# Row maxima, block masks and their spreading matrix padded to 128 on one Trainium2 core

## The chip, the cores and the metric

The kernel runs on one core of a Trainium2 chip. The metric is the time of one execution on the device in microseconds (us), here the median of several runs. The core has five engines that work from queues of their own and wait for each other through semaphores: TensorE (PE; its weight loads are a line of their own, PEld), VectorE (DVE), ScalarE (ACT), GpSimd (POOL) and SyncE (SP), which here only issues transfers (DMA).

## The reference

Inputs are x and ctx, both 8 x 256 x 256 (batch, tokens, width), so 2048 tokens. Four layers follow each other, each added to x:

```python
x = x + softmax(q k^T / sqrt(256)) v          # 16 heads, q = layernorm(x), k = v = ctx
x = x + moe(layernorm(x))                     # 64 experts, 8 per token
x = x + causal_attention(layernorm(x), ctx)   # 16 heads, Wq, Wk, Wv, Wo
x = x + block_ffn(layernorm(x))               # below
```

The last layer has 1024 hidden units in 16 blocks of 64. A router picks 4 of the 16 blocks for each token; hidden units of the others count as zero:

```python
mask = zeros(n, 16).at[rows, top_k(softmax(xf @ router_w.T + router_b), 4)].set(True)
h = relu(where(mask, xf @ w1.T + b1, 0))
y = where(mask, h, 0) @ w2.T + b2
```

## The kernel before

The run has five stages: `prepare` (layer norm and splitting of operands into bf16 parts), a first `attention` ("a0") with the routing of the experts worked in beside it (class `Route`), `experts`, a second `attention` ("a1", causal) with the sum over experts, the query projection and the beginning of the last layer worked in beside it (classes `Combine` and `FirstGroup`), and `finish`, the last layer.

**Attention.** One function builds both. It goes through 16 steps, two per batch, each with 8 heads. For a head PE computes the scores twice: queries by keys (L472, in a1 with a mask added at L475), of which DVE takes the row maxima (L568, in a1 L565), and two steps later keys by queries (L489, L492), from which ACT makes exponentials (L627). The maximum enters this second product as two extra rows of its operand `qst`. For that `cut` on DVE writes the negated maxima of a step as bf16, in a high part (L581) and a rest (L584), into `maxparts`, 16 columns (2 parts of 8 heads) for each half of the queries. PE turns them with two transposes, one per half (`turn_maxima`, L531): the weights are 128 rows by 16 columns, the moving operand is the bf16 identity. The result `max_t` has 16 rows; ACT copies it to `maxrows` (L651), and SP moves it by DMA into `qst`. The two transposes stand in PE's queue after head 4 of each step. PE then multiplies exponentials by values (L512, 32 columns of the array at a time) and turns the outputs (L523). The order of all queues is written out by hand in the functions `step` of each engine; the classes beside the attention hang their work at given heads of given steps.

**The last layer.** The tokens are in four groups of 512. For each group `close_blocks` on DVE (in a1, for the first group, `close`) turns the router's logits into `closed`: 0 for a chosen block and -1e30 for the others, 128 tokens x 16 blocks for each of 4 tiles, fp32. PE turns these with four transposes (`turn_masks`, L1999, and L1799 in a1) into 16 rows in PSUM, which ACT copies to `closed_t` as bf16 (L2056). Then, for each of 8 slices of 128 hidden units, `hidden` adds up in a PSUM bank the products of `w1` with the tokens (L2007; two calls, of which each shows as two fp32 matmuls in the trace) and the product of `spread` with `closed_t` (L2010): `spread` is a 16 x 128 matrix of zeros and ones that gives every hidden unit its block's mask. ACT applies relu with the bias (L2064), and for each tile `output` multiplies by `w2` (L2018). `spread` and the weights are loaded by SP in step 16 of a1 (`FirstGroup.sync`), and every engine of `finish` begins by waiting for them.

Of the kernel before, what the change touches and what calls it, by code (L numbers as in the profile page):

```python
# [7 lines left out]
F32 = mybir.dt.float32  # L8
BF16 = mybir.dt.bfloat16
I32 = mybir.dt.int32  # L10
ALU = mybir.AluOpType
# [3 lines left out]
P = 128  # L15
BATCH, SEQ, D = 8, 256, 256
# [5 lines left out]
HSTEP = HEADS // 2  # L22
# [313 lines left out]
def attention(nc, k, name, q_stack, k_stack, values, scale, causal, out, side):  # L336
# [13 lines left out]
    with ExitStack() as ctx:  # L350
# [10 lines left out]
        maxparts = sb("maxparts", [P, 2, 2, 2, HSTEP], BF16)  # L361
# [9 lines left out]
        max_t = ps[0:2 * HSTEP, 6, SEQ:SEQ + P].bitcast(BF16)  # L371
# [8 lines left out]
        cut_step = sem("cut_step")  # L380
        recips = sem("recips")
# [36 lines left out]
        with nc.Block() as block:  # L418
# [41 lines left out]
            def _(pe):  # L460
# [65 lines left out]
                def turn_maxima(st):  # L526
# [3 lines left out]
                    for j in range(2):  # L530
                        last = pe.transpose(max_t[:, j * P:(j + 1) * P],  # L531
                                            maxparts[:, u % 2, j].rearrange("p a s -> p (a s)"), k.ident_b[:])
# [25 lines left out]
            def _(dve):  # L558
                side.vector_first(dve)
# [11 lines left out]
                def cut(st):  # L571
# [9 lines left out]
                    nc.vector.tensor_copy(maxparts[:, v, :, 0, :], negmax[:, v]).then_inc(cut_step, 1)  # L581
                    per = 3 if causal else 1
                    dve.wait_ge(cut_step, per * h + per)
                    nc.vector.tensor_tensor(maxparts[:, v, :, 1, :], negmax[:, v], maxparts[:, v, :, 0, :], ALU.subtract).then_inc(max_ready, 1)  # L584
# [32 lines left out]
            def _(act):  # L617
# [27 lines left out]
                def copy_maxima(st):  # L645
# [5 lines left out]
                    nc.scalar.copy(maxrows[:, u % 2, :], max_t).then_inc(max_copied, 1)  # L651
# [803 lines left out]
class Combine:  # L1455
# [74 lines left out]
    def gpsimd(self, pool):  # L1530

        pool.wait_ge(self.xn_ready, 4)
# [173 lines left out]
class FirstGroup:  # L1706


    def __init__(self, nc, k, ctx):
# [9 lines left out]
        self.spread = sb("spread", [BLOCKS, FC, P], BF16)  # L1719
# [10 lines left out]
        self.closed = sb("closed", [P, GT, BLOCKS], F32)  # L1730
        self.closed_t = sb("closed_t", [BLOCKS, 2, GT * P], BF16)
        self.early_in, self.w_in = ctx.enter_context(nc.semaphore("ff_early_in")), ctx.enter_context(nc.semaphore("ff_w_in"))

    def attach(self, sem, ps, free, divided):
# [3 lines left out]
        self.masks_ps = ps[0:BLOCKS, :]  # L1738
        self.a_turned, self.a_copied, self.a_ready, self.x_done = sem("ga_turned"), sem("ga_copied"), sem("ga_ready"), sem("gx_done")
        self.own, self.later, self.normal, self.turned, self.copied = sem("g_own"), sem("g_later"), sem("g_normal"), sem("g_turned"), sem("g_copied")  # L1740
        self.logits_ready, self.closing = sem("g_logits"), sem("g_closing")
        self.masks_ready, self.masks_turned, self.masks_copied = sem("g_masks"), sem("g_masks_turned"), sem("g_masks_copied")

    def sync(self, sp, n):
# [6 lines left out]
        if n == 16:  # L1751
            for tile, name in ((self.w1, "w1"), (self.b1, "b1"), (self.spread, "c_spread"), (self.w2, "w2")):
                load(tile, name, self.w_in)
            sp.dma_start(self.b2[:], self.k.dram["b2"].to_broadcast([P, D])).then_inc(self.w_in, 16)
# [108 lines left out]
    def close(self, dve):  # L1863
# [15 lines left out]
        nc.vector.tensor_tensor(self.closed[:], self.others[:], self.logits[:], ALU.is_equal).then_inc(self.closing, 1)  # L1879
# [363 lines left out]
```

## Time and profile before

| | us |
|---|---|
| runs | 1082.7, 1088.0, 1093.1; median 1088.0 |
| the profiled execution, first to last instruction | 1089.6 |
| of it: prepare | to 54 |
| first attention and routing | 54 to 299 |
| experts | 299 to 731 |
| second attention | 731 to 942 |
| last layer (`finish`) | 942 to 1089.6 |

In this execution PE is busy for 932.5 us, its weight loads for 635.0, DVE for 586.8, ACT for 375.0 and POOL for 526.0. A matmul's end is modelled in the profile and reaches into the next matmul, so the pace of PE is read from starts. "Idle before, issue" is time in which an engine waited for nothing that the profile shows.

### The profile page before, as it was taken

To read this page: it belongs to the slowest core of one execution; us is meant where nothing else is said; L and a number is where in the kernel's file an instruction comes from. 1 tells how busy PE (TensorE), PEld (TensorE's weight loads), DVE (VectorE), ACT (ScalarE), POOL (GpSimd) and SP (SyncE) were. 2 spreads that over 40 slices of the span, in tenths; PEclk is the share of its full clock that TensorE was granted. 3 is DMA by queue.
4 is the path that set the end of the run, shared out by engine and by line. 5 is a ranking of instruction groups with operands and counts; after the bars stand their busy time and mean duration, and the time that the engine had idled before them with its cause. 6 is when DMAs were issued, how large, how long until landed. Compare 5 with 4: busy or idle time off the path is not lost. (4 is left out here: it accounts for less than half of the span.)

```text
span 1089.6 us, 20810 instructions
## 1 busy us (share of the span) xinstructions
PE 932.5 (86%) x5679; PEld 635.0 (58%) x5686; DVE 586.8 (54%) x1789; ACT 375.0 (34%) x915; POOL 526.0 (48%) x511
## 2 busy tenths in 40 slices
PE   1188878877599999999999999954689999899998
PEld 1145444545467777777777777732467677465565
DVE  5678898856434444444444444426766867313320
ACT  3446555642322222222222222221245655412211
POOL 4400676776567777777777777722234400201010
PEclk9998898877889999999999999986889999999999
DMA  6764353201576566666666676536876741200000
GB/s 218 224 149 128 82 116 86 56 26 40 190 224 203 180 211 210 203 198 188 195 222 221 206 233 207 180 137 215 238 207 188 197 118 45 84 20 5 15 20 19
DMA packets 78872, 160.80 MB, mean 148 GB/s; under 512 B 18449, under 2 KB 44049, under 8 KB 76481
## 3 DMA queue, kind: packets, MB, share of 16 engines
q1 hardware_dynamic: 59264, 112.23, 35.0%
q0 software_dynamic: 19520, 47.41, 14.0%
q8 instruction: 55, 0.90, 0.4%
q14 instruction: 33, 0.26, 0.1%
HBM read 118.09 MB, written 41.22 MB: 146 GB/s over the span
## 5 line engine op out<-in xcount | busy, mean ns | idle before, releaser
L1318 PE MATMUL ex_ps<-ex_w_gu,ex_rows_t 128*128 x640 | 260.6, 489 | 0.6 <-ACT ex_rows_t L1385 0.6
L1285 POOL DMA_INDIRECT expert_outs<-ex_result,slot_places x160 | 157.5, 985 | 68.4 <-DVE ex_result L1431 55.9
L1280 POOL DMA_INDIRECT ex_rows<-moe_rows,slot_tokens x160 | 154.0, 962 | 55.3 <-issue 48.8
L894 POOL DMA_INDIRECT expert_lists<-rt_number,rt_idx x128 | 124.3, 971 | 102.9 <-DVE rt_idx L995 63.0
L1337 PE MATMUL ex_ps<-ex_w_down,ex_hidden_t 96*128 x640 | 166.5, 382 | 1.0 <-DVE ex_hidden_t L1423 1.0
L1391 ACT ACTIVATE ex_act_g<-ex_ps 128x192 f32<-128x192 f32 x160 | 53.0, 331 | 319.8 <-PE ex_ps L1318 319.8
L627 ACT ACTIVATE a_probs<-a_ps 128x512 f32<-128x512 f32 (+1 forms) x256 | 133.4, 540 | 83.2 <-PE a_ps L489 41.4
L472 PE MATMUL a_ps<-stacked_keys,a_qst 96*128 96x256 bf16 (+1 forms) x512 | 109.5, 286 | 36.7 <-DVE a_negmax L568 11.5
L1431 DVE TENSOR_SCALAR ex_result<-ex_ps,ex_rows 128x256 f32<-128x256 f32 x160 | 77.3, 483 | 94.0 <-PE ex_ps L1337 94.0
L1337 PEld LDWEIGHTS ex_ps<-ex_w_down,ex_hidden_t 96*128 96x128 f32 x640 | 108.6, 190 | 12.0 <-issue 2.3
L1318 PEld LDWEIGHTS ex_ps<-ex_w_gu,ex_rows_t 128*128 128x128 f32 x640 | 109.7, 192 | 9.8 <-issue 1.6
L1417 DVE TENSOR_TENSOR ex_hidden<-ex_act_g,ex_ps 128x192 f32<-128x192 f32 x160 | 56.6, 354 | 107.8 <-ACT ex_act_g L1391 107.8
L489 PE MATMUL a_ps<-a_qst,stacked_keys 98*128 98x256 bf16 (+1 forms) x512 | 105.4, 277 | 4.8 <-DMA a_qst<-a_maxrows 2.5
L568 DVE TENSOR_REDUCE a_negmax<-a_ps 128x2 f32<-128x512 f32 x128 | 84.9, 686 | 24.2 <-PE a_ps L472 23.2
L565 DVE TENSOR_REDUCE a_blockmax<-a_ps 128x3 f32<-128x384 f32 x128 | 70.2, 553 | 48.4 <-PE a_ps L475 48.0
L1951 POOL TENSOR_TENSOR x<-x,ff_b 128x256 f32 (+1 forms) x16 | 11.4, 742 | 159.9 <-DVE ff_xn L2099 85.4
L472 PEld LDWEIGHTS a_ps<-stacked_keys,a_qst 96*128 96x128 bf16 x512 | 48.1, 105 | 66.4 <-issue 29.8
L1423 DVE COPY ex_hidden_t<-ex_ps 96x256 f32<-96x256 f32 x160 | 67.3, 421 | 27.1 <-PE ex_ps L1328 26.1
L1308 PEld LDWEIGHTS ex_ps<-ident,ex_rows 128*128 128x128 f32 x320 | 45.2, 142 | 59.2 <-issue 29.5
L1540 POOL TENSOR_TENSOR gathered<-gathered 128x2048 f32<-128x2048 f32 x6 | 27.1, 4514 | 92.9 <-DMA gathered<-expert_outs 64.0
L1328 PEld LDWEIGHTS ex_ps<-ident,ex_hidden 128*96 128x96 f32 x320 | 39.7, 124 | 53.1 <-issue 31.2
L1308 PE MATMUL ex_ps<-ident,ex_rows 128*128 128x128 f32 x320 | 61.8, 275 | 8.5 <-DMA ex_rows<-moe_rows,slot_tokens 8.5
(248 smaller groups left out, 1402.8 us busy)
## 6 DMA issues: line engine op xcount, KB each, us to landing
ex_w_gu<-in_w_gu_dram SPq DMA_DIRECT2D x64, 384.0 KB, 3.3
gathered<-expert_outs SPq DMA_DIRECT2D x16, 1024.0 KB, 5.9
ex_w_down<-in_w_down_dram SPq DMA_DIRECT2D x64, 192.0 KB, 3.9
a_qst<-q_stack SPq DMA_DIRECT2D x32, 192.0 KB, 4.4
stacked_keys<-k_stack SPq DMA_DIRECT2D x32, 192.0 KB, 4.5
a_qst<-q_stack SPq DMA_DIRECT2D x32, 128.0 KB, 4.3
stacked_keys<-k_stack SPq DMA_DIRECT2D x32, 128.0 KB, 4.0
k_stack<-split_parts SPq DMA_DIRECT2D x8, 384.0 KB, 2.6
```

The costliest lines, as they stand in the source:

```text
L472: last = pe.matmul(bank[:, at:at + keys], qst[0:ROWS, u, s, j * P:(j + 1) * P], kst[0:ROWS, u, s, 0:keys], start=True, stop=True)
L489: last = pe.matmul(bank[:, at:at + SEQ - first], kst[:, u, s, j * P:(j + 1) * P], qst[:, u, s, first:SEQ], start=True, stop=True)
L565: nc.vector.tensor_reduce(blockmax[:, u % 2, s, :], ps[:, QK_BANKS[s % 3], 0:cols].rearrange("p (b n) -> p b n", n=P), AX.X, ALU.max, nega ...
L568: nc.vector.tensor_reduce(negmax[:, u % 2, :, s], ps[:, QK_BANKS[s % 3], :].rearrange("p (j n) -> p j n", j=2), AX.X, ALU.max, negate=True ...
L627: nc.scalar.activation(probs[:, s, 0:cols], ps[:, 2 + s % 2, 0:cols], ACT.Exp, scale=scale).then_inc(exped, 1)
L894: nc.gpsimd.indirect_dma_start(k.lists, bass.IndirectOffsetOnAxis(ap=self.idx[:, t, s:s + 1], axis=0), self.number[:, t, s:s + 1], None).t ...
L1280: nc.gpsimd.indirect_dma_start(rows[:, t % R, :], None, k.xn.rearrange("t p d -> (t p) d"), bass.IndirectOffsetOnAxis(ap=k.ids[:, begin + ...
L1285: nc.gpsimd.indirect_dma_start(k.outs, bass.IndirectOffsetOnAxis(ap=k.places[:, begin + t:begin + t + 1], axis=0), result[:, t % R], None) ...
L1308: last = pe.transpose(ps[:, j % 2, c * P:(c + 1) * P], rows[:, j, c * P:(c + 1) * P], k.ident[:])
L1318: last = pe.matmul(ps[:, 2 + j % 2, 0:2 * FF], rows_t[:, j % 2, c * P:(c + 1) * P], w_gu[:, bass.ds(ring, 1), c, :].rearrange("p a n -> p ...
L1337: last = pe.matmul(ps[:, 6 + j % 2, 0:D], hidden_t[:, j % 2, c * P:(c + 1) * P], w_down[:, bass.ds(ring, 1), c, :].rearrange("p a n -> p ( ...
L1431: nc.vector.tensor_scalar(result[:, j], ps[:, 6 + j % 2, 0:D], rows[:, j, bass.ds(expert + D, 1)], None, ALU.mult).then_inc(one.result_rea ...
```

## The change

Three small operands of PE are widened to 128 with zeros; what is computed stays the same.

- `maxparts` gets 128 columns for each half, of which 16 are used; the transposes at L531 have weights of 128 x 128 and write 128 rows of PSUM. ACT still copies 16. DVE clears `maxparts` at the start of each attention and waits for that.
- `closed` gets 128 columns per tile, so that the mask transposes are 128 x 128, and `closed_t` 128 rows, all of which ACT copies. POOL clears `closed` at the start of the second attention; DVE waits for it in `close`.
- `spread` gets 128 rows, so that the matmul at L2010 has 128 x 128 weights and a 128 x 512 moving operand. POOL clears it; SP waits for that and loads the 16 rows with the values after `w2` instead of before it.

```diff
-        maxparts = sb("maxparts", [P, 2, 2, 2, HSTEP], BF16)
+        maxparts = sb("maxparts", [P, 2, 2, P], BF16)
-        max_t = ps[0:2 * HSTEP, 6, SEQ:SEQ + P].bitcast(BF16)
+        max_t = ps[:, 6, SEQ:SEQ + P].bitcast(BF16)
@@ turn_maxima
                         last = pe.transpose(max_t[:, j * P:(j + 1) * P],
-                                            maxparts[:, u % 2, j].rearrange("p a s -> p (a s)"), k.ident_b[:])
+                                            maxparts[:, u % 2, j], k.ident_b[:])
@@ attention, vector
+                nc.vector.memset(maxparts[:], 0.0).then_inc(maxparts_clear, 1)
+                dve.wait_ge(maxparts_clear, 1)
                 side.vector_first(dve)
@@ cut
-                    nc.vector.tensor_copy(maxparts[:, v, :, 0, :], negmax[:, v]).then_inc(cut_step, 1)
+                    nc.vector.tensor_copy(maxparts[:, v, :, 0:HSTEP], negmax[:, v]).then_inc(cut_step, 1)
@@ copy_maxima
-                    nc.scalar.copy(maxrows[:, u % 2, :], max_t).then_inc(max_copied, 1)
+                    nc.scalar.copy(maxrows[:, u % 2, :], max_t[0:2 * HSTEP]).then_inc(max_copied, 1)
@@ Combine.gpsimd
+        self.nc.gpsimd.memset(self.first.closed[:], 0.0).then_inc(self.first.closed_clear, 1)
+        self.nc.gpsimd.memset(self.first.spread[:], 0.0).then_inc(self.first.closed_clear, 1)
         pool.wait_ge(self.xn_ready, 4)
@@ FirstGroup
-        self.spread = sb("spread", [BLOCKS, FC, P], BF16)
+        self.spread = sb("spread", [P, FC, P], BF16)
-        self.closed = sb("closed", [P, GT, BLOCKS], F32)
-        self.closed_t = sb("closed_t", [BLOCKS, 2, GT * P], BF16)
+        self.closed = sb("closed", [P, GT, P], F32)
+        self.closed_t = sb("closed_t", [P, 2, GT * P], BF16)
-        self.masks_ps = ps[0:BLOCKS, :]
+        self.masks_ps = ps
@@ FirstGroup.sync
         if n == 16:
-            for tile, name in ((self.w1, "w1"), (self.b1, "b1"), (self.spread, "c_spread"), (self.w2, "w2")):
+            for tile, name in ((self.w1, "w1"), (self.b1, "b1"), (self.w2, "w2")):
                 load(tile, name, self.w_in)
+            sp.wait_ge(self.closed_clear, 2)
+            load(self.spread[0:BLOCKS], "c_spread", self.w_in)
@@ close and close_blocks (there without the wait)
+        dve.wait_ge(self.closed_clear, 1)
-        nc.vector.tensor_tensor(self.closed[:], self.others[:], self.logits[:], ALU.is_equal).then_inc(self.closing, 1)
+        nc.vector.tensor_tensor(self.closed[:, :, 0:BLOCKS], self.others[:], self.logits[:], ALU.is_equal).then_inc(self.closing, 1)
```

## Rows read from the trace of the kernel before

**Rows 1.** The chain of work that ended last, from 700 us, shares by line

```profile
by line: PE ff_ps L2007 15.1%; PE ff_ps L2018 14.5%; PE ff_ps L2010 2.6%; PE ff_ps L1975 2.2%; PE ff_ps L1992 1.3%; PE ff_ps L1984 0.7%; PE ff_ps L1967 0.5%; PE ff_ps L1999 0.3%; DVE ff_y L2124 0.1%; issue 0.0%; DVEq L2123 0.0%
```

**Rows 2.** Stretches: busy us (count) of PE, PEld, DVE, ACT, POOL; clock, DMA share, GB/s

```profile
132.00:145.30 13.30, 10.52 (x85) 5.95 (x86) 12.45 (x47) 7.25 (x17) 8.65 (x9) 0.87 0.48 82
...
848.00:856.40 8.40, 6.46 (x79) 5.09 (x79) 8.09 (x32) 4.04 (x10) 0.00 (x0) 1.00 0.79 206
890.00:930.00 40.00, 38.07 (x456) 29.47 (x455) 26.53 (x90) 23.58 (x60) 0.00 (x0) 1.00 0.23 62
...
943.00:1072.80 129.80, 129.80 (x484) 76.61 (x482) 31.54 (x131) 29.67 (x54) 10.39 (x15) 1.00 0.04 13
```

**Rows 3.** Timeline around L2010; start, us, engine, line, count, idle before

```profile
953.67 0.19 PEld L2007 LDWEIGHTS ff_ps<-ff_xn_t,ff_w 128*128 128x128 f32 x1 [0.24 <-issue]
954.10 0.19 PEld L2007 LDWEIGHTS ff_ps<-ff_xn_t,ff_w 128*128 128x128 f32 x1 [0.24 <-issue]
954.53 0.59 PE L2007 MATMUL ff_ps<-ff_xn_t,ff_w 128*128 128x512 f32 x1
955.05 0.09 PEld L2010 LDWEIGHTS ff_ps<-ff_closed_t,ff_spread 16*128 16x128 bf16 x1 [0.76 <-issue]
955.37 0.30 PEld L2007 LDWEIGHTS ff_ps<-ff_xn_t,ff_w 128*128 128x128 f32 x2 [0.23 <-issue]
...
955.90 0.19 PEld L2007 LDWEIGHTS ff_ps<-ff_xn_t,ff_w 128*128 128x128 f32 x1 [0.24 <-issue]
```

**Rows 4.** The matmuls of L2010: count, ns shortest/median/longest, first and last start

```profile
L2010 PE MATMUL ff_ps<-ff_closed_t,ff_spread x32: 384/384/385, 943.9 to 1072.4; 16*128 16x512 bf16 x32
```

**Rows 5.** Timeline: a bf16 matmul of full size and its follower

```profile
845.34 0.39 PE L1635 MATMUL a_ps<-cb_parts,cb_minus 128*128 128x512 bf16 x1
...
845.57 0.22 PE L472 MATMUL a_ps<-stacked_keys,a_qst 96*128 96x128 bf16 x1
```

**Rows 6.** Timeline around a pair of maxima transposes, with and without them between

```profile
891.96 0.22 PE L492 MATMUL a_ps<-mask_kq,ident_b 128*128 128x128 bf16 x1
...
892.11 0.28 PE L531 MATMUL a_ps<-ident_b,a_maxparts 128*16 128x128 bf16 x2
892.32 0.10 PEld L472 LDWEIGHTS a_ps<-stacked_keys,a_qst 96*128 96x128 bf16 x1
...
892.85 0.22 PE L492 MATMUL a_ps<-mask_kq,ident_b 128*128 128x128 bf16 x1
...
892.91 0.22 PE L472 MATMUL a_ps<-stacked_keys,a_qst 96*128 96x128 bf16 x1
```

**Rows 7.** Busy us (count) of L531 alone by stretch; clock, DMA share, GB/s

```profile
815.00:890.00 75.00, 1.95 (x14) 0.68 (x14) 0.98 0.64 173
890.00:930.00 40.00, 1.39 (x10) 0.49 (x10) 1.00 0.23 62
```

**Rows 8.** The matmuls of L531, and who waited for them (us, times)

```profile
L531 PE MATMUL a_ps<-ident_b,a_maxparts x64: 219/222/314, 61.8 to 927.3; 128*16 128x128 bf16 x64
...
  ACT a_maxrows L651: 34.9, 25
```

**Rows 9.** Timeline: four mask transposes and the matmul after them

```profile
976.41 0.60 PE L1999 MATMUL ff_ps<-ident,ff_closed 128*16 128x128 f32 x4
...
976.85 1.88 PE L2007 MATMUL ff_ps<-ff_xn_t,ff_w 128*128 128x512 f32 x4
```

**Rows 10.** Timeline: when DVE is done with what PE turns next

```profile
974.87 0.19 DVE L2116 TENSOR_SCALAR ff_closed<-ff_closed 128x64 f32<-128x64 f32 x1
...
996.28 2.20 DVE L2099 TENSOR_SCALAR ff_xn<-x,ff_moments,ff_rstd 128x256 f32<-128x256 f32 x4
...
1002.45 0.60 PE L1984 MATMUL ff_ps<-ident,ff_xn 128*128 128x128 f32 x4
```

**Rows 11.** A memset; POOL's first sum by line: busy, mean ns, idle before, releasers

```profile
55.50 0.37 POOL L882 MEMSET rt_blank<- 128x320 f32 x1
...
L1540 POOL TENSOR_TENSOR gathered<-gathered 128x2048 f32<-128x2048 f32 x6 | 27.1, 4514 | 92.9 <-DMA gathered<-expert_outs 64.0 <-DVE cb_xn L1577 28.9
```

## What the change will do to the time

> **What bounds the kernel now.** I read the chain of work that ended last first, then busy times by stretch, and then the timeline of single instructions around each edited line. The chain, asked for from 700 us to the end at 1089.6 us, is work of TensorE (PE) in the last feed-forward stage (`finish`) nearly throughout; the spread matmul (L2010) has 2.6% of these 390 us in it, 10 us [rows 1]. The stretches tell where PE's time is the kernel's time [rows 2]: from 943 to 1072.8 us, within `finish`, PE is busy in all of 129.8 us, at granted clock 1.00, so what PE saves there shortens the run one for one. From 890 to 930 us (end of the second attention) PE is busy 38.1 of 40 us and VectorE (DVE) 26.5. But from 132 to 145.3 us (first attention) DVE is busy 12.45 of 13.3 us and from 848 to 856.4 us 8.09 of 8.4, while PE is busy 10.5 and 6.5: there DVE sets the pace and time saved on PE is waited away. The experts' stage between the attentions isn't touched.
>
> **The change, part by part.**
>
> *The spread matmul, 32 times [rows 3, 4].* Before, its weights are 16x128 and its moving operand 16x512 bf16, among fp32 matmuls of 128x128 weights. Read the stream in starts, since the ends of matmuls are modelled and overlap. Inside the fp32 stream loads and matmuls follow each other every 0.43 us (loads at 953.67 and 954.10, matmul at 954.53), and each load lies under the matmul before it. Three things break the rhythm around L2010. Its weight load should begin by 954.53 + 0.43 = 954.96 at the latest and begins at 955.05: 0.09 us lost. The PE load engine had been idle 0.76 us by then, with nothing to wait for ("issue"), so the load was held back and not late. From 955.05 to the next start at 955.37 pass 0.32 us, where the stream of a full-size bf16 matmul with the same 512 columns takes 0.23 us (L1635 at 845.34, the next matmul at 845.57 [rows 5]): 0.09 us lost on the load of L2010 that lay bare. And after it the load and the first fp32 matmul start together, and the next load in the rhythm comes 0.53 us later instead of 0.43: 0.10 us. Together 0.28 us; taking the bf16 stream as 512 columns over 2.4 GHz (granted clock 1.00), 0.21 us, it would be 0.30. With 128 rows, L2010 has the array shape of its neighbours, as L1635 has of L472, and I take all three parts as gone: 0.29 x 32 = 9.3 us, bounds 9.0 and 9.6. PE is the whole path here, so it is 9.3 us of the run, if the others keep up.
>
> The Trainium skill, "TensorEngine Tiling (Array Packing)", section Key Properties, says that changing the tiling mode drains TensorE. By its rule the gap belongs to every change between a narrow and a full shape; applied to the mask transposes too it would add eight changes in `finish`. The trace agrees for L2010 but not for those transposes (next but one).
>
> *The transposes of the row maxima, 32 pairs [rows 6 to 8].* Before, 128x16 weights in bf16. The first of a pair starts 0.15 us after the matmul before it (891.96 to 892.11), where the same predecessor is otherwise followed after 0.06 (892.85 to 892.91): 0.09 us. The pair plus what follows takes 0.21 us (892.11 to 892.32) where two full 128-column bf16 instructions take 0.12: 0.09, and about 0.01 in the rhythm after. Padded to 128 columns the pair has its neighbours' shape; the full-size bf16 loads of L492 and L475 are hidden at the same spacing of 0.06, so I charge nothing for eight times as many columns. That is 0.19 x 32 = 6.1 us of PE time, the upper bound. How much is on the path? The second attention has 16 pairs. Of the first four I expect nothing: that stretch starts up and waits for loads. After 890 us PE is the bound: five pairs, which pass. Between 815 and 890 us lie seven [rows 7]. There every other step ends in a DVE-bound stretch like that from 848 to 856 us, with a pair inside it that gains nothing, and the pair of the step between passes on to DVE, which waits for PE then: four pass. I count 9 x 0.19 = 1.7 us. In the first attention DVE is busy over 90% in the stretch shown, and the rest has waits for ScalarE (ACT) and DVE; ACT waited for these transposes 25 times in both attentions [rows 8], so half of the gap (the 0.09 before it) can reach it. I take 16 pairs at 0.04, 0.7 us, with bounds 0 and 3. Attention together: 2.4 us, bounds 0 and 6.1.
>
> The Trainium skill, "TensorE: Matmul & The Clock Gate", section LDWEIGHTS, gives a weight load as its columns over 1.2 GHz. By that rule, an estimate, 16 to 128 columns cost 0.09 us more per load, 6 us over 64 loads, if nothing hid them, and the attention's gain would be nil. The 0.06 us spacing of full-size loads speaks against it.
>
> *The transposes of the expert-block masks, 16, fp32 [rows 9].* They are narrow as well (128x16), yet four take 0.44 us (976.41 to 976.85), 0.11 each, the pace of a full fp32 transpose, and the following full-size L2007 starts on time. Nothing is lost there, so padding gains nothing: 0 us, at most 4 x 0.1.
>
> *Copies and vector operations.* ACT's copies of masks and maxima keep their elements per partition. DVE's writes into the padded tiles (L581, L584, L2115, L2116 and their like in `close`) keep their elements and only lie further apart. In `finish` the last of them ends at 975.06 and PE turns the masks at 976.41: 1.3 us of cover. Without it each 0.1 us would delay one of three groups. The four operations at L2099 end at 998.48 and PE needs them at 1002.45: 4.0 us of cover [rows 10]; steps shortened by 4 x 0.29 take 1.2 of it. What is late next is therefore still PE.
>
> *Memsets and waits [rows 11].* GpSimd (POOL) clears `closed` (512 fp32 per partition) and `spread` (1024 bf16), before its first sum in the second attention. 320 fp32 took 0.37 us, so 512 some 0.6; the second at most twice that; 1.8 us, under the 28.9 us for which POOL waited for DVE there. DVE clears `maxparts` (512 bf16) at the start of each attention; under 0.5 us by the same row. In the second its first work is a sum of gathered rows, for which a transfer must land first. In the first nothing as long is there, so up to 0.5 us may show. Uncovered, both together would be 2.3 us. SyncE's (SP's) new wait, at step 16 of the second attention, is for memsets at its start; queued behind it are only the loads of `spread` and `b2`, whose waiters start after the attention. The spread load changes place with `w2` and is the same 32 KB. DVE's new wait in `close` is likewise long fulfilled. I charge 0.
>
> **Sum**: 9.3 + 2.4 + 0 - 0 = 11.7 us. Against the profiled execution's 1089.6 us that gives 1077.9. The median of the runs, 1088.0 (1082.7 to 1093.1), lies 1.6 below it, so the forecast is 1076.3 us.
>
> **Rivals.** (1) *The maxima's gain arrives in full*: 9.3 + 6.1 = 15.4, 1072.6 us. For it: ACT waits on these transposes [rows 8], and everything after the attention shifts with it. Against: the DVE-bound stretches [rows 2]. (2) *Only `finish` gains*; DVE, ACT and the DMA waits absorb the rest, or longer loads eat it: 9.3, 1078.7 us. For it: first attention. Against: 890 to 930 us. (3) *The change doesn't remove the gap*: it belongs to the change between bf16 and fp32 and not to the shape. Then nothing is gained: 1088 us. For it: both neighbours of L2010 are fp32 [rows 3]. Against: L531 stands between bf16 matmuls and pays too [rows 6]. (4) *Slower, by the clock*: PE, a little less busy in the attentions, is granted 1.2 GHz more often; the stretch from 132 us already shows 0.87. At 1.2 instead of 2.4 GHz the streaming takes twice as long, so each microsecond of PE-bound run at the lower level costs 0.5. It decides from 2 x 11.7 = 23 us more at 1.2 GHz on; with 40 us more the time would be 1088 + 20 - 11.7 = 1096. Against: 1.00 from 890 us on with PE busy 95%, and only 6.1 us of activity goes away.
>
> **How the numbers follow.** Forecast 0.60, (1) 0.12, (2) 0.17, (3) 0.07, (4) 0.04. A single case is uncertain by its bounds and by how far executions differ, some 4 us. The range takes the forecast, (1) and (2), each with that margin: 1072.6 - 4 to 1078.7 + 4.5, about 1068.5 to 1083.2; outside lie (3), (4) and little else. About 1% (10.9 us, 1077.1) is what a measurement of this kernel can tell from no change. My forecast is only just beyond: it falls under 1077.1 with 0.6, (1) with 0.85, (2) with 0.35: 0.36 + 0.10 + 0.06 = 0.52. Slower by over 1% only in part of (4): 0.03. The rest, 0.45, is within 1%.
>
> **What the profile after would show.** L2010 128x128 with its load hidden and idle "issue" before it gone; from one L2010 to the next (2.23 us before) about 1.94; `finish` shorter by 9 us with PE still busy throughout. L531 following its predecessor after 0.06 us. The mask transposes unchanged at 0.11. The second attention shorter by 1 to 3 us, the first by less than 1. If L2010's load still starts after the matmul before it, (3) holds; a lower mean clock in the attentions shows (4); the forecast is also wrong if a wait of PE for ACT's relu or for DVE's L2099 appears in `finish`.

## The result, and the profile after

The changed kernel took 1076.3 us (median of 4 runs, 1072.9 to 1077.6); the kernel before 1085.4 us (median of 4 runs, 1082.7 to 1093.1: the three from which the forecast started and one of 1082.7 more). The ratio is 0.9886, 95% interval 0.9847 to 0.9924: faster by about 1.1%. The forecast was 1076.3 us, 1.1% faster, range 1068.5 to 1083.2. In the experiments below the same kernel was timed again against 24 runs of the one before: 1077.5 us, ratio 0.9900, interval 0.9865 to 0.9935, or 10.9 us of 1089.65.

The profiled execution took 1074.2 us, 15.4 less than that of before. It is split here by stage, each time read as the start of the stage's first PE instruction in the two timelines (the third stage ends, and the fourth begins, with the last expert matmul):

| stage | before, us | after, us | difference |
|---|---|---|---|
| up to the first attention | 54.0 | 53.3 | 0.7 |
| first attention and routing | 245.4 | 242.7 | 2.7 |
| experts | 423.2 | 423.6 | -0.4 |
| last expert matmul to `finish` | 219.4 | 216.5 | 2.9 |
| `finish` | 147.6 | 138.1 | 9.5 |

The chain of work that ended last, from 700 us, shares by line (the spread matmul is L2019 now, L2016 the first layer, L2027 the second, L1984 the output projection):

```profile
by line: PE ff_ps L2016 14.9%; PE ff_ps L2027 14.8%; PE ff_ps L1984 1.8%; PE ff_ps L2019 1.5%; PE ff_ps L2001 1.4%; PE ff_ps L1993 0.7%; PE ff_ps L1976 0.6%; PE ff_ps L2008 0.3%; DVE ff_y L2133 0.1%; issue 0.1%; DVEq L2132 0.0%
```

L2019 has 1.5% where L2010 had 2.6% [rows 1]. The rest of the chain is the same work of PE.

Stretches of the kernel after; busy us (count) of PE, PEld, DVE, ACT, POOL, then granted clock, DMA share, GB/s:

```profile
884.40:924.40 40.00, 37.81 (x459) 29.90 (x459) 26.57 (x90) 23.34 (x60) 0.00 (x0) 1.00 0.26 63
937.00:1057.50 120.50, 120.18 (x478) 80.13 (x483) 31.61 (x131) 29.69 (x54) 10.41 (x15) 1.00 0.04 14
```

PE is busy in practically all of `finish` as before [rows 2], with 478 matmul records in 120.5 us where 484 stood in 129.8 (a few records are missing in each). So what went was time inside PE's stream, and nothing else took its place.

Timeline of the kernel after around L2019: start, us, engine, line, operation, tiles, and the idle time before it with what ended it:

```profile
942.34 0.19 PEld L2016 LDWEIGHTS ff_ps<-ff_xn_t,ff_w 128*128 128x128 f32 x1 [0.24 <-issue]
942.77 0.19 PEld L2016 LDWEIGHTS ff_ps<-ff_xn_t,ff_w 128*128 128x128 f32 x1 [0.24 <-issue]
943.20 0.10 PEld L2019 LDWEIGHTS ff_ps<-ff_closed_t,ff_spread 128*128 128x128 bf16 x1 [0.24 <-issue]
...
945.13 0.10 PEld L2019 LDWEIGHTS ff_ps<-ff_closed_t,ff_spread 128*128 128x128 bf16 x1 [0.24 <-issue]
...
945.55 0.38 PE L2019 MATMUL ff_ps<-ff_closed_t,ff_spread 128*128 128x512 bf16 x1
...
945.77 1.88 PE L2016 MATMUL ff_ps<-ff_xn_t,ff_w 128*128 128x512 f32 x4
```

The load of L2010 that follows the one at 955.05 [rows 3], in the kernel before:

```profile
957.28 0.09 PEld L2010 LDWEIGHTS ff_ps<-ff_closed_t,ff_spread 16*128 16x128 bf16 x1 [0.76 <-issue]
```

Read the loads: 942.34, 942.77, 943.20, each 0.43 us behind the last. The load of L2019 is now in the rhythm, with 0.24 us of idle time before it where L2010's had 0.76 [rows 3], and so it lies under the matmul before. The next fp32 matmul starts 0.22 us after L2019 (945.55 to 945.77), the pace of a bf16 stream of 512 columns. From one L2019 to the next pass 1.93 us (943.20 to 945.13), before 2.23 (955.05 to 957.28). All 32 loads are like that: "issue" before L2019 is 7.6 us over 32, where it was 24.3. The matmul itself is as long as before, 379 ns against 384 [rows 4]. What was saved was around it:

```profile
L2019 PEld LDWEIGHTS ff_ps<-ff_closed_t,ff_spread x32: 97/98/98, 937.4 to 1056.7; 128*128 128x128 bf16 x32
L2019 PE MATMUL ff_ps<-ff_closed_t,ff_spread x26: 378/379/380, 939.8 to 1057.2; 128*128 128x512 bf16 x26
L1536 POOL MEMSET ff_spread<- x1: 952/952/952, 728.5 to 728.5; 128x1024 bf16 x1
...
  issue: 7.6, 32
```

(Those are the instructions of the tile `spread`: count, ns shortest/median/longest, first and last start. The records of 6 of the 32 matmuls are missing; the loads are complete.)

The other edited lines, in the same form:

```profile
L532 PE MATMUL a_ps<-ident_b,a_maxparts x64: 216/218/315, 61.0 to 921.3; 128*128 128x128 bf16 x64
...
L560 DVE MEMSET a_maxparts<- x2: 272/272/272, 53.4 to 728.1; 128x256 uint32 x2
...
  ACT a_maxrows L654: 32.6, 25
```

The memsets of `maxparts` took 0.27 us each, those of `spread` and `closed` on POOL 0.95 and 0.53 us at 728 us, and nothing in the profile waits for them. The maxima transposes (L532) follow their predecessor after 0.05 us (834.62 to 834.67, below) where they followed it after 0.15 [rows 6]. Their weight loads, now of 128 columns instead of 16, have a median of 97 ns instead of 88, and lie hidden. So the 0.09 us more per load that the prediction set against the change, as an estimate from the columns, didn't come. Four mask transposes (L2008) hand over to L2016 after 0.43 us, as [rows 9] has 0.44:

```profile
968.05 0.60 PE L2008 MATMUL ff_ps<-ident,ff_closed 128*128 128x128 f32 x4
...
968.48 1.88 PE L2016 MATMUL ff_ps<-ff_xn_t,ff_w 128*128 128x512 f32 x4
```

### The profile page after: what moved, and what is told of

It reads as the page before. It is cut to its first block and busy times, and to the rows that moved or that the text cites. A ratio compares the mean times of both kernels' runs of the same rounds, so it can differ in the third digit from the quotient of the medians.

```text
span 1074.2 us, 20810 instructions
## 1 busy us (share of the span) xinstructions
PE 914.4 (85%) x5673; PEld 638.9 (59%) x5686; DVE 591.1 (55%) x1791; ACT 374.1 (35%) x915; POOL 526.7 (49%) x513
## 5 line engine op out<-in xcount | busy, mean ns | idle before, releaser
L513 PE MATMUL a_ps<-a_probs,a_v_aug 128*32 128x256 f32 (+1 forms) x1024 | 67.3, 384 | 0.0
```

## Experiments

The theory: TensorE loses about 0.09 us on each side whenever it goes between a full instruction and one with few rows or columns, and the padding takes that away; where PE is the bound it is time of the run. The rivals: the gap belongs to the change of type; the maxima's gain arrives in full; something else in the change (memsets, loads in another order, tiles in other places) makes the difference; the clock. Ratios are to the kernel before on the same chip, with 95% intervals; one without an interval is a single run. `finish` is its length in the profiled execution.

**Everything again.** `e1_all` is the changed kernel itself.

> The whole change, beside its parts on the same chip. Theory (the gap around narrow operands goes): 11 to 13 us faster than before, ratio about 0.989; last stage 9.4 us shorter. Rival (the full 6.1 us of the maxima arrive): 15 us, ratio 0.986.

1077.46 us, 0.9900 (0.9865 to 0.9935). `finish` 138.1 us.

**The spread matmul alone.** `closed_t` and `spread` have 128 rows, the transposes of masks and maxima stay narrow. The unused rows of `closed_t` are cleared once.

```diff
-        self.spread = sb("spread", [BLOCKS, FC, P], BF16)
+        self.spread = sb("spread", [P, FC, P], BF16)
-        self.closed_t = sb("closed_t", [BLOCKS, 2, GT * P], BF16)
+        self.closed_t = sb("closed_t", [P, 2, GT * P], BF16)
...
+        self.nc.gpsimd.memset(self.first.closed_t[:], 0.0).then_inc(self.first.closed_clear, 1)
...
```

> Only the spread matmul has 128 rows; mask transposes and maxima stay 128x16, the unused rows of closed_t are cleared once by POOL. Theory: 9.4 us faster, ratio 0.991; last stage 138.1 us as with the whole change, since the fp32 mask transposes cost nothing even when narrow; maxima still start 0.09 us late. Rival (every narrow shape drains, as the mode rule reads): last stage about 1 us longer than with the whole change, because 3 groups of mask transposes keep two gaps each. Rival (type change, not shape): the gap around the spread matmul stays and nothing is gained.

1078.25 us, 0.9902 (0.9867 to 0.9936): the whole of the change within the measurement. `finish` 138.14 us, to a hundredth what the full change has. The mask transposes are narrow here and full there, so padding them is worth nothing.

**The maxima alone.** Only what the diff does to `maxparts`; `closed`, `closed_t` and `spread` are as before.

> Only the transposes of the maxima are padded to 128 columns. Theory: their gaps of 0.19 us per pair go in the trace, 6.1 us of TensorE time, but 2 to 3 us of the run, ratio 0.998. Rival 1 (all arrives): 6 us, ratio 0.9945. Rival 2 (all absorbed by DVE, ACT and DMA): ratio 1.000. Last stage as before, 147.6 us.

1088.28 us, 0.9998 (0.9976 to 1.0020): nothing that can be measured. `finish` 147.6 us, as before.

**A control.** All tiles, memsets, waits and the order of loads as in the change, but each matmul and copy takes only the 16 rows or columns of before, so that only what the array is given differs from `e1_all`.

```diff
...
-                    pe.matmul(bank, spread[:, m, :], closed_t[:, f % 2, :], start=False, stop=True).then_inc(hid_ready, 1)
+                    pe.matmul(bank, spread[0:BLOCKS, m, :], closed_t[0:BLOCKS, f % 2, :], start=False, stop=True).then_inc(hid_ready, 1)
...
```

> Tiles, memsets, waits and the order of loads as in the changed kernel, but TensorE's operands are narrow again (16 of the 128). Theory: all gaps are back, time as before within 0.3%, ratio 1.000; last stage 147.6 us. Rival (memsets or order of loads matter): 1 to 2 us slower than before, or part of the gain stays.

1089.78 us, 1.0002 (0.9979 to 1.0025), and 2.23 us from one spread matmul to the next. So the memsets, the waits and the other order change nothing that can be measured (the interval is 2.5 us to either side); the gain is the shape. In its profiled execution `finish` took 149.2 us and not 147.6. The stretches tell why; first `e4_control`, then the same place of `e3_maxima` (columns as above):

```profile
935.60:940.10 4.50, 4.42 (x7) 1.51 (x8) 3.97 (x17) 0.69 (x1) 2.76 (x4) 0.63 0.00 0
```

```profile
932.10:936.60 4.50, 4.41 (x10) 1.54 (x10) 3.97 (x17) 0.69 (x1) 2.77 (x4) 1.00 0.00 0
```

Some 3.4 us at the start of `finish` ran at 1.2 GHz in one (mean granted clock 0.63) and at 2.4 GHz in the other: 1.6 us longer. The attentions of this control were 242.4 and 215.1 us, as short as those of the changed kernel (242.7 and 216.5) without any of its padding. A microsecond or three of a stage's difference between two profiled executions says nothing here. That holds for the 2.7 and 2.9 us of the attentions in the table of stages too: the first attention lasted 240.4 to 244.7 us in five kernels with full pairs of maxima transposes (96 columns counted in) and 240.9 to 245.6 in seven with narrow ones.

**How many rows.** The change with 64 rows and columns in use, and with 96.

```diff
...
-                    pe.matmul(bank, spread[:, m, :], closed_t[:, f % 2, :], start=False, stop=True).then_inc(hid_ready, 1)
+                    pe.matmul(bank, spread[0:64, m, :], closed_t[0:64, f % 2, :], start=False, stop=True).then_inc(hid_ready, 1)
...
```

> All three operands 64 wide instead of 128 (64 rows of the spread matmul, 64 columns of the transposes). Theory (the array has shapes of 32, 64 and 128, a change of shape costs the gap): the spread matmul keeps its pitch of 2.23 us, last stage 147.6 us, maxima start 0.15 us after their predecessor. Rival (what counts is how few rows or columns are loaded): gaps shrink with width, pitch between 1.94 and 2.23.

> All three operands 96 wide. Theory: 96 counts as full, as the 96-row operands of the attention scores do, which follow 128-row ones without a gap; pitch 1.93 us, last stage 138.1 us, maxima 0.06 us after their predecessor, as with 128. Rival (gaps shrink with width): pitch about 2.0.

64: 1084.14 us (one run), `finish` 147.7, timeline:

```profile
946.76 0.19 PEld L2016 LDWEIGHTS ff_ps<-ff_xn_t,ff_w 128*128 128x128 f32 x1 [0.24 <-issue]
947.71 0.09 PEld L2019 LDWEIGHTS ff_ps<-ff_closed_t,ff_spread 64*128 64x128 bf16 x1 [0.76 <-issue]
...
949.95 0.09 PEld L2019 LDWEIGHTS ff_ps<-ff_closed_t,ff_spread 64*128 64x128 bf16 x1 [0.76 <-issue]
```

96: 1080.21 us (one run), `finish` 138.3, timeline:

```profile
951.17 0.10 PEld L2019 LDWEIGHTS ff_ps<-ff_closed_t,ff_spread 96*128 96x128 bf16 x1 [0.24 <-issue]
...
953.11 0.10 PEld L2019 LDWEIGHTS ff_ps<-ff_closed_t,ff_spread 96*128 96x128 bf16 x1 [0.24 <-issue]
```

With 64 rows the engine idles the full 0.76 us before the load and the pitch is 2.24 us, as with 16, and in the second attention the maxima's transposes with 64 columns come 0.15 us after their predecessor, as with 16; with 96 it is in the rhythm and the pitch 1.94, as with 128. The type is bf16 among fp32 in both. The gap is thus a step between 64 and 96 rows. The Trainium skill, "TensorEngine Tiling (Array Packing)", section Key Properties, says that changing the tiling mode drains TensorE, and its section Available Configurations lists modes of 32, 64 and 128 rows: 96 rows fit only the last. The two rows above agree.

**Type instead of shape.** The spread matmul is fp32 like its neighbours and keeps 16 rows; the mask transposes are bf16 with 16 columns (the mask's large negative value is rounded to bf16, and `closed_t` is a single buffer, to fit).

```diff
-        self.spread = sb("spread", [P, FC, P], BF16)
+        self.spread = sb("spread", [P, FC, P], F32)
-        self.closed = sb("closed", [P, GT, P], F32)
-        self.closed_t = sb("closed_t", [P, 2, GT * P], BF16)
+        self.closed = sb("closed", [P, GT, P], BF16)
+        self.closed_t = sb("closed_t", [P, 1, GT * P], F32)
...
```

> All operands narrow as before, but with their types exchanged: spread matmul in fp32 (16 rows), mask transposes in bf16 (16 columns). Theory (shape decides, fp32 transposes being run at full shape whatever their width): the fp32 spread matmul still has about 0.1 us lost before and after it although its neighbours are fp32 too, and the bf16 mask transposes now start about 0.1 us late and delay what follows by 0.1. Rival (the gap belongs to the change of type): fp32 spread matmul without a gap.

1119.8 us (one run), `finish` 174.6. The whole time says nothing of the gap, because a matmul in fp32 costs more by itself: the pitch is 2.96 us, 0.73 more than 2.23, and 32 x 0.73 = 23 us. (`finish` also began with some 7 us at 1.2 GHz here, granted clock 0.59.) The timeline does tell:

```profile
1035.73 1.02 PE L2016 MATMUL ff_ps<-ff_xn_t,ff_w 128*128 128x512 f32 x2
...
1036.68 0.29 PEld L2019 LDWEIGHTS ff_ps<-ff_closed_t,ff_spread 16*128 16x128 f32 x2 [0.76 <-issue]
...
1037.73 0.51 PEld L1984 LDWEIGHTS ff_ps<-ff_wo,ff_ao_t 128*128 128x128 f32 x3 [0.76 <-issue]
```

```profile
1031.00 0.38 PE L2027 MATMUL ff_ps<-ff_w,ff_hidden_t 128*128 128x256 f32 x1
1031.31 0.39 PE L2008 MATMUL ff_ps<-ident_b,ff_closed 128*16 128x128 bf16 x4
...
1031.63 1.12 PE L2016 MATMUL ff_ps<-ff_xn_t,ff_w 128*128 128x512 f32 x2
```

All is fp32 around L2019, and the idle time before its first load is 0.76 us still; and so is that before the full-size instruction behind it. The spread matmul's first record starts 0.52 us after the one before it in the timeline, where the stream has 0.43. So the change of type is not the cause. One thing stays open: the two fp32 records of one L2019 start 0.53 us apart, 0.10 more than the stream's 0.43, though both are narrow. So a slice of hidden units loses 0.38 us here (2.96 against six times 0.43) and not 0.30.

The mask transposes, narrow in bf16, now start 0.31 us after their predecessor, where full-size instructions of that line have 0.22, and what follows them 0.15 us after the last of them, where full-size bf16 transposes have 0.06: in bf16 they pay 0.09 on each side, as the maxima do, while in fp32 of the same 128x16 they paid nothing [rows 9]. The Trainium skill, "TensorEngine Tiling (Array Packing)", Gotcha 2, has it that column tiling excludes the transpose mode for fp32 inputs on this chip. That would explain the exception, since such a transpose could then not leave the full mode; no run here shows that it is the reason. It isn't fp32 as such: the products of exponentials and values (L512, 32 columns, fp32, no transposes) come late too. The kernel before:

```profile
894.04 0.22 PE L492 MATMUL a_ps<-mask_kq,ident_b 128*128 128x128 bf16 x1
...
894.19 0.86 PE L512 MATMUL a_ps<-a_probs,a_v_aug 128*32 128x256 f32 x16
```

They start 0.15 us after the full-size L492, as the maxima do. Of the 64 groups of L512 in the run 16 follow L492 like this, and so they do in the kernel after (L513), since the change leaves them narrow.

**The maxima's gap, five times.** Both kernels turn the maxima five times over, in one pair after another (the last pair's result is used). In `e5_pairs_narrow` the pairs alternate between 16 and 128 columns, which makes six changes of shape out of two; in `e6_pairs_wide` all are full.

```diff
-                    for j in range(2):
-                        last = pe.transpose(max_t[:, j * P:(j + 1) * P],
-                                            maxparts[:, u % 2, j], k.ident_b[:])
+                    for turn in range(5):
+                        wide = P if turn % 2 else 2 * HSTEP
+                        for j in range(2):
+                            last = pe.transpose(max_t[0:wide, j * P:(j + 1) * P],
+                                                maxparts[:, u % 2, j, 0:wide], k.ident_b[:])
```

> The changed kernel with each pair of maxima transposes issued five times to the same place, narrow (16 columns), wide, narrow, wide, narrow. Against the next kernel it has six gaps of about 0.095 us more in each of 32 steps, 18 us of TensorE time. Theory (PE bounds part of the attention, as forecast: 2.4 of 6.1 us arrive): 7 us slower than the all-wide kernel. Rival 1 (the gaps of the attention are absorbed by DVE, ACT and DMA, as the run with padded maxima alone suggests): 0 to 3 us slower. Rival 2 (all arrives): 18 us slower.

> As the kernel above, all five pairs wide: eight more full-size bf16 instructions of 0.06 us in each of 32 steps, 15 us of TensorE time without a gap. Theory (2.4 of 6.1 us arrive, a share of 0.4): about 6 us slower than the changed kernel, so about 0.995 of the kernel before. Rival 1 (absorbed): as the changed kernel, 0.989. Rival 2 (all arrives): 1.003.

Alternating: 1096.78 us, 1.0068 (1.0044 to 1.0093). All full: 1081.05 us, 0.9928 (0.9899 to 0.9957). The timeline of `e5_pairs_narrow` (a row with x10 stands for all ten transposes):

```profile
847.86 0.22 PE L493 MATMUL a_ps<-mask_kq,ident_b 128*128 128x128 bf16 x1
848.01 0.95 PEld L534 LDWEIGHTS a_ps<-ident_b,a_maxparts 128*16 128x16 bf16 x10
848.01 1.13 PE L534 MATMUL a_ps<-ident_b,a_maxparts 128*16 128x128 bf16 x10
849.07 0.23 PE L473 MATMUL a_ps<-stacked_keys,a_qst 96*128 96x128 bf16 x1
```

From predecessor to follower pass 1.21 us (847.86 to 849.07), where eleven spacings of full-size instructions at 0.056 make 0.61: 0.60 us for six changes, 0.10 each. Over 32 steps that is 19.2 us of PE time, and the two medians lie 15.7 us apart. Four fifths arrive: the theory's 7 us missed, and rival 2 was nearer. Of the 14 us (32 x 8 x 0.056) that `e6_pairs_wide` adds to `e1_all`, about 3.6 arrive by the medians, a quarter, where the theory had 6; the two intervals overlap, so this share is rough. And of the single pair's 6.1 us nothing measurable did. The first microseconds are swallowed, the later ones pass: slack is used up. Where, the next section shows.

**Where a pair's gain goes.** In the causal attention ACT's copy of the maxima stands ahead of the work of the next stage that ACT does at the same place. These two kernels put it behind, one with the full change (`e9_reorder`), one with `e2_spread` (`e10_reorder_narrow`).

```diff
-                        if s == 3 and scores(after(st, -1)):
+                        if s == 3 and not causal and scores(after(st, -1)):
                             copy_maxima(after(st, -1))
...
                         side.scalar(act, st, s)
+                        if s == 3 and causal and scores(after(st, -1)):
+                            copy_maxima(after(st, -1))
```

> The changed kernel with one move on ScalarE in the second attention: the copy of the maxima (head 3) comes after the side work of that head instead of before it, so that the projection's high part no longer waits for the transposes of the maxima. Theory (in every other step TensorE waits for ScalarE's high part, which is queued behind the copy of the maxima; that wait begins where the transposes end and swallows the gap behind them): TensorE's wait of 0.58 us after the maxima goes in these steps, their pitch falls from 9.50 us to 9.0 to 9.4, the second attention gains 1 to 4 us, ratio to before 0.986 to 0.989. Rival (VectorE sets these steps): pitch stays 9.50, ratio as the changed kernel.

> The same move, with narrow transposes of the maxima (only the spread matmul is padded). Theory: with ScalarE's wait out of the way both gaps of a pair count, so the steps that were 9.60 us narrow and 9.50 us padded now differ by 0.19 us between this kernel and the one before it. Rival (VectorE takes over at once): they differ by 0.1 or less.

`e9_reorder`: 1076.0 us, 0.9880 (0.9853 to 0.9906), which can't be told from `e1_all`'s 0.9900. The 1 to 4 us that were expected of the second attention don't show. `e10_reorder_narrow`: 1078.8 us (one run). The lengths of the second attention's steps, from one pair of maxima transposes to the next in the timelines, us (steps numbered from 0 over both attentions, so 16 to 31 are the second's):

| step | before | `e2_spread` | `e3_maxima` | after | `e10`, narrow | `e9`, full | `e6`, five full | `e5`, alternating |
|---|---|---|---|---|---|---|---|---|
| 20, 22, 24, 26 | 9.60 | 9.60 | 9.50 | 9.50 | 9.18 | 8.97 | 9.95 | 10.46 |
| 21 | 10.28 | 10.27 | 10.27 | 10.28 | 10.27 | 11.32 | 10.28 | 10.76 |
| 28 | 9.01 | 9.01 | 8.81 | 8.81 | 9.01 | 8.81 | 9.26 | 9.86 |
| 29 | 9.91 | 9.91 | 9.81 | 9.81 | 9.66 | 9.46 | 10.26 | 10.76 |
| 30 | 7.30 | 7.30 | 7.21 | 7.21 | 7.30 | 7.21 | 7.65 | 8.15 |

These lengths repeat to 0.01 us from one profiled execution to another, of this kernel and of others with the same pairs, in nearly all cases (the first four steps and numbers 23 and 27 do not, and are left out), so they resolve what the whole times can't. With a full pair steps 20, 22, 24 and 26 are 0.10 us shorter, although the pair's gap was 0.19; steps 28, 29 and 30 are 0.20, 0.10 and 0.09 shorter; steps 21 and 25 not at all. Together 4 x 0.10 + 0.39 = 0.8 us. In the steps left out no gain shows either: the first four together take 40.19 us at the shortest with narrow pairs (`e4_control`) and 40.33 with full ones (the kernel after), and from the last pair to `finish` it is 14.78 us before and 14.79 after.

In step 21 PE waits for DVE's row maxima, and the wait takes up the gap; first the kernel before, then the one after:

```profile
835.32 0.22 PE L472 MATMUL a_ps<-stacked_keys,a_qst 96*128 96x128 bf16 x1 [0.79 <-DVE a_blockmax L565]
```

```profile
828.21 0.21 PE L473 MATMUL a_ps<-stacked_keys,a_qst 96*128 96x128 bf16 x1 [0.89 <-DVE a_blockmax L568]
```

The kernel before, timeline at the start of step 22, one of the four:

```profile
841.88 0.28 PE L531 MATMUL a_ps<-ident_b,a_maxparts 128*16 128x128 bf16 x2
...
842.19 0.36 ACT L651 COPY a_maxrows<-a_ps 16x256 bf16<-16x256 bf16 x1 [1.38 <-PE a_ps L531]
...
842.46 0.57 ACT L1672 CAST cb_parts<-a_ps 128x512 bf16<-128x512 f32 x1
...
843.08 0.10 PEld L1635 LDWEIGHTS a_ps<-cb_parts,cb_minus 128*128 128x128 bf16 x1 [0.43 <-ACT cb_parts L1672]
...
843.31 0.22 PE L472 MATMUL a_ps<-stacked_keys,a_qst 96*128 96x128 bf16 x1 [0.48 <-DVE a_blockmax L565]
```

The same place after:

```profile
834.62 0.22 PE L493 MATMUL a_ps<-mask_kq,ident_b 128*128 128x128 bf16 x1
...
834.67 0.27 PE L532 MATMUL a_ps<-ident_b,a_maxparts 128*128 128x128 bf16 x2
...
834.98 0.36 ACT L654 COPY a_maxrows<-a_ps 16x256 bf16<-16x256 bf16 x1 [1.28 <-PE a_ps L532]
835.25 0.57 ACT L1677 CAST cb_parts<-a_ps 128x512 bf16<-128x512 f32 x1
...
835.87 0.10 PEld L1640 LDWEIGHTS a_ps<-cb_parts,cb_minus 128*128 128x128 bf16 x1 [0.53 <-ACT cb_parts L1677]
836.10 0.22 PE L473 MATMUL a_ps<-stacked_keys,a_qst 96*128 96x128 bf16 x1 [0.58 <-DVE a_blockmax L568]
```

ACT has been waiting for the transposes (1.38 us); it copies the maxima, then casts `parts` for the stage beside the attention, and PE's next load, L1635, waits for that cast (0.43 us). So from the transposes' start to the next head's first matmul it is a chain over ACT, and it takes 1.43 us before (841.88 to 843.31) and 1.43 after (834.67 to 836.10). What lies ahead of the transposes, 0.09, passes on. What lies behind them on PE, 0.10, becomes a longer wait, 0.53 instead of 0.43. (The last row's release is put down to DVE. The matmul of L1635, after L1640, has no record in either timeline, and its load waits for ACT.)

If that is right, taking the copy out of the chain must let the other half through. `e9_reorder`, timeline at the start of step 20, of the same kind:

```profile
816.21 0.59 ACT L1679 CAST cb_parts<-a_ps 128x512 bf16<-128x512 f32 x1 [0.65 <-PE a_ps L1636]
...
816.53 0.27 PE L532 MATMUL a_ps<-ident_b,a_maxparts 128*128 128x128 bf16 x2
...
816.84 0.36 ACT L654 COPY a_maxrows<-a_ps 16x256 bf16<-16x256 bf16 x1
...
817.15 0.10 PEld L1642 LDWEIGHTS a_ps<-cb_parts,cb_minus 128*128 128x128 bf16 x1
...
817.42 0.22 PE L473 MATMUL a_ps<-stacked_keys,a_qst 96*128 96x128 bf16 x1
```

The cast runs first, the load of L1642 has no wait, and the next head comes after 0.89 us instead of 1.43. Full against narrow pairs now differ by 9.18 - 8.97 = 0.21 us in these steps and 9.66 - 9.46 = 0.20 in step 29: the whole gap. So it is shown where the half went. The reordering's own 0.53 us per step is given back in part in the steps between, 21 and 25, which grew from 10.28 to 11.32 and 10.60 us (PE's wait for DVE's row maxima in step 21 is 1.75 us instead of 0.89); the whole is no faster.

The table also explains why the first microseconds are swallowed and later ones pass. `e5` is longer than `e6` by 0.51 us in steps 20 to 26: the 0.09 ahead of the transposes and 0.41 between them, while the 0.10 behind is again swallowed; and step 21, which gave nothing back for a single pair, grows by 0.48. There PE's wait for DVE is used up. In the first attention the step length that occurs most is 9.85 or 9.86 us in every one of these kernels, even `e5` (DVE is busy for 9.3 of it); of the steps that repeat only the third moved with the padding, from 7.63 to 7.54.

**Per matmul or per change of shape?** The kernel before, with the spread matmuls of two slices put one behind the other, so that 32 narrow matmuls make 32 changes of shape instead of 64.

```diff
-                    if m == 0:
+                    if m % 2 == 0:
+                        return
+                    if m == 1:
                         wait(pe, masks_copied, f)
-                    pe.matmul(bank, spread[:, m, :], closed_t[:, f % 2, :], start=False, stop=True).then_inc(hid_ready, 1)
+                    for n in (m - 1, m):
+                        bank = ps[:, 2 + (FC * f + n) % HBANKS, :]
+                        pe.matmul(bank, spread[:, n, :], closed_t[:, f % 2, :], start=False, stop=True).then_inc(hid_ready, 1)
```

> The kernel before, all narrow, with the spread matmuls of two slices of hidden units issued one after the other, so that the array's shape changes 32 times instead of 64 in the last stage. Theory (the loss is per change of shape): 16 x 0.29 us less, last stage 142.9 us, ratio 0.996. Rival (the loss is per narrow matmul): 147.6 us, ratio 1.000.

1087.35 us, 0.9979 (0.9957 to 1.0001). Two slices take 4.16 us instead of 4.46 (twice 2.23), 0.30 less: one narrow matmul's whole loss for one pair of changes saved. In bf16 the loss is per change and not per narrow matmul. Its timeline and the list of who waited for what in `finish` (us in total, times, longest):

```profile
1059.82 0.11 PEld L2014 LDWEIGHTS ff_ps<-ff_closed_t,ff_spread 16*128 16x128 bf16 x2 [0.76 <-issue]
...
1060.35 0.30 PEld L2007 LDWEIGHTS ff_ps<-ff_xn_t,ff_w 128*128 128x128 f32 x2 [0.42 <-issue]
```

```profile
PE ff_ps L1975 <- ACT ff_ao_t L2051: 3.3, 4, 0.8
```

Both spread loads stand in one row behind a single 0.76 us. But of 16 x 0.30 = 4.8 us only some 1.5 are left over, since `hid_ready` now comes late for the first of two slices, ACT gets behind, and PE waits 3.3 us for its copies; in the profiled execution a stretch at 1.2 GHz at the start of `finish` (granted clock 0.62 over 4.5 us) took these too (`finish` 148.2). Padding does the same without moving any work.

## Why the prediction was right, step by step

**The spread matmul: right, size and mechanism.** 9.3 us forecast (bounds 9.0 and 9.6); `finish` became 9.46 us shorter, 147.60 to 138.14, 0.296 us for each of the 32, and 138.14 came out in `e1_all`, `e2_spread` and `e10_reorder_narrow` alike. The three parts that were read out of the rhythm (load held back, load bare, first interval longer) all went. The load is hidden, the pitch 1.93 and PE busy throughout, as the signs had it, and no wait of PE for another engine appears in `finish`.

**Rival 3, type instead of shape: refuted** by `e7_64` and `e8_96`, in which the type is the same and only the rows differ, and by `e11_types`, in which the gap stays with all neighbours in fp32.

**The maxima: the mechanism right, the term too large.** Forecast 2.4 us; the steps that repeat show 0.8 in the second attention and 0.1 in the first, about 0.9. The size of the gap was right (0.60 us for six changes is 0.20 a pair, forecast 0.19), and so was where DVE swallows it. The step that failed is "five pairs, which pass" and "four pass", each counted at the full 0.19: PE busy 38.1 of 40 us was taken for PE setting the pace at every instant. But in the four, and in step 29, the half of the gap behind the transposes runs into PE's wait for ACT's cast, which stands in the rows above (0.43 us), and only 0.10 passes. Step 30 gained only 0.09 as well, but the moved copy didn't bring the rest back there, so its other half went elsewhere, which wasn't followed. The 9 x 0.19 = 1.7 us became 4 x 0.10 + 0.20 + 0.10 + 0.09. For the first attention, "16 pairs at 0.04" was 0.1 instead of 0.7 as far as its steps repeat; those of 9.86 us kept their length. The sign "the first by less than 1" can't be read from the stages: their difference is 2.7 us, and the control's first attention is 3.0 us shorter with narrow pairs.

**Mask transposes, memsets, waits, the order of loads: right at 0.** (The prediction speaks of eight changes of shape around the mask transposes in `finish`; only three of the four groups stand there, so it is six.) `finish` is 138.14 us with and without full mask transposes; the control with all of these is at 1.0002 (0.9979 to 1.0025). The two POOL memsets took 1.5 us against the 1.8 allowed.

**Together.** By mechanism 9.5 + 0.9 = 10.4 us, against 11.7 forecast; repeated measurement gives 10.9, with an interval from 7 to 15. That lies about midway between the forecast and rival 2 (only `finish` gains, 9.3), and the whole times can't tell those two apart; the step lengths can, and say that the attention gains, but less than half of what was forecast. That the median met the forecast to a tenth of a microsecond is chance: one more run lowered the kernel before by 2.6 us, and the difference of the two medians is 9.0 us, not 11.7. **Rival 1** (all 6.1 us of the maxima) is refuted by `e3_maxima`, 0.9998: 6.1 us would be 0.9944, outside its interval. **Rival 4**, the clock, shows nowhere: the mean granted clock is 0.941 after and 0.940 to 0.948 in `e4_control` and `e3_maxima`, and before and after it is 0.86 from 54 to 300 us and 0.88 from 721 to 942. About 5 us of the 15.4 between the two profiled executions are not the change's at all, as the control's attention shows. In the second attention they lie in the steps that don't repeat: the first four took 44.5 us before, 40.3 after and 40.2 in the control with its narrow pairs, and step 23 gave 1.8 back (11.15 before, 12.95 after). The granted clock doesn't explain it, being the same; the cause stays open.

## What to carry to other kernels

Look in the timeline for an instruction whose weight load is held back by "issue" and lies bare, among others of full size that are hidden: if it uses 64 or fewer rows or columns, and isn't an fp32 transpose, zero-padding its operands to the neighbours' shape costs a memset and gave 0.3 us per occurrence here where TensorE is the bound. Before counting on it, follow what stands behind the narrow instruction: if the next one waits for another engine that was waiting for this one, only the part ahead of it is gained. When stages differ by less than the run's variation, compare single steps that repeat to 0.01 us, and make a control that has everything of the change but its effect.

## What was not expected of the hardware

- The gap has a threshold and no slope: 16 and 64 rows lose the same 0.30 us (pitch 2.23 and 2.24), 96 and 128 rows nothing (1.94 and 1.93).
- It is paid per change between narrow and full, about 0.10 us for each in bf16 transposes (0.60 for six), and not per narrow instruction: two adjacent narrow bf16 matmuls lost 0.30 us together. (The two fp32 records of a narrow matmul lost 0.10 us between them as well, which is open.)
- Narrow transposes of 128x16 pay it in bf16 (0.09 on each side) and not in fp32 (0.11 us each, follower on time). Narrow fp32 products that aren't transposes pay too (L512, 0.15 us after a full-size bf16 instruction instead of 0.06).
- The weight loads of these bf16 transposes don't grow with their columns: median 88 ns for 16, 109 for 64, 123 for 96 and 97 for 128 (`before`, `e7_64`, `e8_96`, after).
- A stretch at 1.2 GHz may fall on the first microseconds of `finish` in one execution and not in another (granted clock 0.63 against 1.00 over 4.5 us), for 1.6 us of the run. It did in five of the fourteen profiled executions (`e4_control`, `e5_pairs_narrow`, `e9_reorder`, `e11_types`, `e12_two_slices`).
